# Row sums of a sliding attention by matrix products, and its outputs scaled after the product with the values

## The chip, the cores and the metric

The kernel runs on one core of a Trainium2 chip. The metric is the device time of one execution in microseconds (us), the median of several runs. A core has five engines with a queue of instructions each, which are worked off in order: PE (TensorE, matrix products into the PSUM banks, with PEld for its weight loads), DVE (VectorE), ACT (ScalarE), POOL (GpSimd) and SP, which only issues transfers. An engine waits for another through semaphores: `wait_ge(G["name"], n)` holds the queue until the counter `name` has come to n, and `.then_inc(G["name"], 1)` counts it up when an instruction is done.

## The reference, cut to what matters

The kernel computes a decoder of two layers on x of 4 batches x 256 tokens x 256 features. Only the first step of the first layer is changed, a causal attention over a sliding window, with 16 heads of width 16:

```python
qkv = x @ w_qkv.T                       # then split into q, k, v: 16 heads x 16
diff = C + qa[:, None] - ka[None, :]    # C = WINDOW = 64, keys of the chunk before and of this one
base = (diff >= 0) & (diff <= WINDOW)
scores = jnp.einsum('bhncd,bhnkd->bhnck', qc, kc) * SCALE
scores = jnp.where(mask[None, None], scores, -jnp.inf)
attn = jax.nn.softmax(scores, axis=-1)
out = jnp.einsum('bhnck,bhnkd->bhncd', attn, vc)
o = out.transpose(0, 2, 1, 3).reshape(B, S, E)
return o @ w_out.T
```

Behind it come the sum with x and a layer norm, an attention over a context of 1601 rows (below: stage B), a quantised feed-forward, and the second layer.

## The kernel before, in words

**Tiling.** The sliding attention is cut into 16 groups n = 0 to 15. Batch b has four of them, n = 4b + i, where i stands for half f of the heads (8 heads) and half t of the tokens (128 tokens). One group is a tile `sm[:, n % 4]` of 128 queries x 8 heads x 128 keys in single precision (fp32). Four such tiles are kept, and two tiles `PT` of turned weights.

**One group before the change.** PE's `a_scores(n)` writes the scores into banks 0 to 3. DVE's `a_mask(n)` adds the mask and moves them to `sm`, and `a_max(n)` takes the negated row maxima. ACT takes eight exponentials in place, one for each head, each with `accum_out` for its row sums. DVE's `a_rinv(n)` inverts the sums, and POOL multiplies the 128 x 1024 weights by them. PE's `a_transpose(n)` turns them into banks 4 and 5; DVE (i = 0 and 3) or ACT (i = 1 and 2) copies them to `PT` in `a_weightsT(n)`; PE's `a_output(n)` multiplies them with the values into bank 7.

**Once a batch.** ACT's `a_outT(b)` copies bank 7 to `oT`. PE's `a_project_out(b)` multiplies it with the output weights, again into bank 7. DVE's `a_ln(b)` adds x and takes the statistics; POOL's `rstd_of` raises the variance to the power -0.5; DVE's `ln_end` scales. PE's `a_query`, `a_key` and `a_value` project the next batch, and `to_xT` turns the normed rows.

**Order.** All engines run a loop over n written out by hand; what stands in an engine's queue has its turn in that order. DVE's loop before is

```python
a_mask(n)
if n >= 1:
    a_rinv(n - 1)
a_max(n)
if n >= 2 and not on_act(n - 2):
    a_weightsT(n - 2)
if i == 3 and b > 0:
    a_ln(b - 1)
```

so the maxima of group n stand behind the inversion for group n - 1, which waits for its eight exponentials. PE runs the scores of n, a projection, the output of n - 3 and the transposes of n - 2. Behind the loop PE projects the queries, keys and values of stage B, while ACT and DVE split the context into a high and a low part (`c_split`); then come the scores of stage B with DVE's `b_max`, ACT's `b_exp` and so on.

Of the kernel before, what the change touches and what calls it, by code (L numbers as in the profile page):

```python
# [39 lines left out]
P = 128  # L40
# [98 lines left out]
def build(nc, d, xs, ys, out):  # L139
    with ExitStack() as ctx:  # L140
# [120 lines left out]
        def w_qrT(h):  # L261
# [102 lines left out]
        rsum = sb("rsum", [P, 4, H0F])  # L364
        rinv = sb("rinv", [P, 4, H0F])
# [12 lines left out]
            a_q a_k a_v a_q_sb a_k_sb a_v_sb a_vmix a_s a_add a_max a_exp a_rinv a_norm  # L378
            a_pt a_pt_act a_pt_dve a_o a_o_sb a_y a_y_sb ld_rest
            b_q b_k b_v hi_part lo_part c_Thi c_Tlo c_Rhi c_Rlo wk_split b_s b_max b_exp b_t b_pt_hi b_pt b_o b_o_sb b_ot b_ot_sb b_y  # L380
            x_k x_neg x_exp x_kf x_kf_hi x_kf_lo x_m1 x_m1_sb x_m1T x_m1T_sb x_kv x_kvbd
# [53 lines left out]

        def on_act(n):

            return n % GROUPS in (1, 2)
# [8 lines left out]
        def _(sp):  # L447
# [31 lines left out]
            sp.wait_ge(G["const_set"], 6)  # L479
# [72 lines left out]
        def _(pool):  # L552
# [4 lines left out]
            g.memset(mhalf[:, :], -0.5).then_inc(G["const_set"], 1)  # L557

# [23 lines left out]
            def a_mixed_values(b):  # L582
# [3 lines left out]
                pool.wait_ge(G["a_norm"], GROUPS * b + 1)  # L586
                for j, (w, lo, hi) in enumerate(((1, 0, WIN), (0, WIN, P))):
                    g.tensor_copy(real(2, lo, hi), real(w, lo, hi)).then_inc(G["a_vmix"], 1)
                    pool.wait_ge(G["a_vmix"], 2 * b + j + 1)

            for n in range(NG):
# [78 lines left out]
            def r_scatter(b, parts):  # L670
                pool.wait_ge(G["r_rows"], 2 * b + 2)
                pool.wait_ge(G["ln_done"], 4 * NT + 2 * b + 2)
                if b == 0:
                    pool.wait_ge(G["const_set"], 10)
# [50 lines left out]
        def _(act):  # L725
# [47 lines left out]
            for n in range(NG):  # L773
                b, i = divmod(n, GROUPS)
                act.wait_ge(G["a_max"], n + 1)
                for h in range(H0F):
                    a.activation(sm[:, n % 4, h, :], sm[:, n % 4, h, :], ACT.Exp, bias=mx[:, n % 4, h:h + 1],  # L777
                                 accum_out=rsum[:, n % 4, h:h + 1]).then_inc(G["a_exp"], 1)
# [6 lines left out]
                if i == 1:  # L785
                    if b > 0:
                        a_outT(b - 1)
# [47 lines left out]
            def x_exp(n):  # L835
# [6 lines left out]
                a.activation(low, PS[KBANKS[c % 4]][:, 0:words], ACT.Relu, scale=-1.0).then_inc(G["x_neg"], 1)  # L842
                act.wait_ge(G["x_neg"], n + 1)
# [29 lines left out]
            for b in range(B):  # L873
                if b > 0:
                    b_oT(2 * b - 1)
                if b == 0:
                    a_outT(B - 1)
# [1728 lines left out]
```

## Time and profile before

| | |
|---|---|
| median of 3 runs | 735.99 us (735.14 to 736.39) |
| the profiled execution, its own time | 735.17 us |
| its span in the profile | 733.3 us |
| busy share of the span: PE, PEld, DVE, ACT, POOL | 89%, 73%, 66%, 59%, 27% |
| groups of the sliding attention: first scores to the first scores of stage B | 10.7 to 97.07 us |
| mean granted TensorE clock of the whole execution | 0.968 of full speed |

The span runs from the first to the last instruction that the profiler saw; the execution's own time is 1.9 us more. A row of a timeline gives the start, the duration, the engine, the line and what was written and read; in square brackets stands how long the engine had idled before it and who released it. Neighbouring instructions of an engine overlap by some tens of ns, so what one of a row of them costs is read from start to start. An fp32 matrix product is recorded as two or more instructions. All of PE's instructions have the line of a helper, so they are told apart by shapes: `32*128 32x256` are scores of an even group (t = 0), `32*64 32x256` of an odd one, `cst,arena 128*128 128x128` eight transposes, `128*32 128x128` the output of an even group, `128*32 128x64` of an odd one.

### The profile page before, as it was taken

To read this page: it belongs to the slowest core of one execution; us is meant where nothing else is said; L and a number is where in the kernel's file an instruction comes from. 1 tells how busy PE (TensorE), PEld (TensorE's weight loads), DVE (VectorE), ACT (ScalarE), POOL (GpSimd) and SP (SyncE) were. 2 spreads that over 40 slices of the span, in tenths; PEclk is the share of its full clock that TensorE was granted. 3 is DMA by queue.
4 is the path that set the end of the run, shared out by engine and by line. 5 is a ranking of instruction groups with operands and counts; after the bars stand their busy time and mean duration, and the time that the engine had idled before them with its cause. 6 is when DMAs were issued, how large, how long until landed. Compare 5 with 4: busy or idle time off the path is not lost.

```text
span 733.3 us, 13912 instructions
## 1 busy us (share of the span) xinstructions
PE 650.4 (89%) x4832; PEld 534.9 (73%) x4833; DVE 486.5 (66%) x1091; ACT 435.2 (59%) x1124; POOL 201.6 (27%) x354
## 2 busy tenths in 40 slices
PE   7798787998998999978989999999978799999950
PEld 5566677998998899864567788888865388787840
DVE  2577777469478478448877857666556577777725
ACT  4998856358357368356878747465342356566612
POOL 2455520032000000001233444344127222222315
PEclk9999899999999999998999999999999999999985
DMA  8997000220230232410020000000195201111114
GB/s 298 383 321 219 1 1 1 90 91 1 91 91 0 91 103 103 136 37 1 1 87 1 2 1 2 1 1 1 43 427 213 65 30 51 50 50 50 49 58 138
DMA packets 32226, 62.03 MB, mean 85 GB/s; under 512 B 2500, under 2 KB 26824, under 8 KB 29928
## 3 DMA queue, kind: packets, MB, share of 16 engines
q1 hardware_dynamic: 30152, 56.04, 22.6%
q0 software_dynamic: 2016, 5.22, 2.0%
q8 instruction: 36, 0.59, 0.4%
q14 instruction: 22, 0.18, 0.1%
HBM read 45.80 MB, written 15.55 MB: 84 GB/s over the span
## 4 chain that ended last, share of the span: by engine, by line
PE 68%; DVE 12%; ACT 12%; issue 3%; POOL 2%; DMA 2%; SPq 0%; POOLq 0%; ACTq 0%; DVEq 0%
PE banks L1783 45%; PE bank L1783 23%; ACT arena L777 4%; DVE U_split L1253 3%; ACT U_split L796 2%; DVE mx L1207 1%; DVE wabs L1386 1%; DMA ys<-arena 1%; POOL rstd L574 1%; ACT xT L731 1%; ACT arena L842 1%; DMA w_qkv<-in_w_qkv 1%; DVE fh L1436 1%; ACT arena L950 1%; ACT arena L997 0%
## 5 line engine op out<-in xcount | busy, mean ns | idle before, releaser
L1783 PE MATMUL banks<-U_split 128*128 128x512 f32 (+1 forms) x616 | 146.7, 350 | 5.9 <-DVE U_split L1253 3.9
L1783 PE MATMUL bank<-U_split 128*128 128x256 f32 (+1 forms) x864 | 113.1, 287 | 12.4 <-DVE U_split L1253 11.7
L1783 PEld LDWEIGHTS bank<-U_split 128*128 128x128 f32 x864 | 106.7, 191 | 15.7 <-issue 7.5
L1783 PEld LDWEIGHTS banks<-U_split 128*128 128x128 f32 x616 | 96.5, 190 | 23.6 <-issue 7.9
L796 ACT ACTIVATE U_split<-arena 128x1024 fp32r (+6 forms) x122 | 97.1, 822 | 22.0 <-DVE arena L1344 11.1
L1783 PE MATMUL banks<-cst,arena 128*128 128x128 f32 (+1 forms) x594 | 90.6, 280 | 6.1 <-DVE arena L1215 3.1
L1783 PE MATMUL banks<-arena 128*128 (+4 forms) x632 | 85.3, 386 | 4.8 <-DVE arena L1201 3.9
L571 POOL TENSOR_SCALAR rstd<-mv 128x1 f32<-128x1 f32 x38 | 10.8, 285 | 263.2 <-DVE mv L1185 239.8
L1783 PEld LDWEIGHTS banks<-cst,arena 128*128 128x128 f32 (+1 forms) x594 | 69.7, 143 | 18.5 <-POOL arena L602 3.7
L1783 PEld LDWEIGHTS banks<-arena 64*128 64x128 f32 (+3 forms) x632 | 61.5, 178 | 22.5 <-issue 7.6
L1043 ACT ACTIVATE arena<-banks,dmx 128x128 f32<-128x128 f32 (+1 forms) x128 | 52.8, 423 | 38.6 <-DVE dmx L1540 38.6
L647 POOL TENSOR_SCALAR arena<-arena,dri 128x128 f32<-128x128 f32 (+1 forms) x128 | 52.0, 425 | 75.3 <-DVE dri L1511 75.3
L1253 DVE TENSOR_TENSOR w_x_split<-arena,U_split 128x1024 fp32r<-128x1024 f32 x46 | 56.1, 1222 | 22.8 <-ACT U_split L796 22.8
L1783 PE MATMUL banks<-w_x_split,U_split 128*128 128x256 f32 (+2 forms) x196 | 66.1, 337 | 0.0
L796 ACT ACTIVATE U_split<-banks 128x512 fp32r<-128x512 f32 (+2 forms) x67 | 32.4, 505 | 54.5 <-PE banks L1783 54.5
L1253 DVE TENSOR_TENSOR U_split<-arena,U_split 128x512 fp32r<-128x512 f32 (+5 forms) x76 | 55.5, 752 | 2.3 <-ACT U_split L796 2.1
L777 ACT ACTIVATE arena<-arena,mx 128x128 f32<-128x128 f32 x128 | 49.5, 391 | 9.5 <-DVE mx L1207 9.5
L1253 DVE TENSOR_TENSOR U_split<-banks,U_split 128x512 fp32r<-128x512 f32 (+2 forms) x63 | 35.2, 571 | 27.2 <-ACT U_split L796 27.2
L713 POOL DMA_INDIRECT ys<-arena x23 | 26.2, 1140 | 95.3 <-ACT arena L1112 88.8
L1783 PE MATMUL bank<-arena 128*32 128x64 f32 (+4 forms) x672 | 46.2, 290 | 4.0 <-DVE arena L1215 1.8
L1783 PEld LDWEIGHTS bank<-arena 128*32 128x32 f32 (+2 forms) x672 | 29.3, 127 | 19.3 <-issue 5.6
L602 POOL TENSOR_TENSOR arena<-arena,rinv 128x1024 f32<-128x1024 f32 x16 | 30.4, 1899 | 43.8 <-DVE rinv L1211 43.8
(239 smaller groups left out, 1187.5 us busy)
## 6 DMA issues: line engine op xcount, KB each, us to landing
arena<-in_w_exp SPq DMA_DIRECT2D x8, 1536.0 KB, 14.1
xs<-arena SPq DMA_DIRECT2D x8, 1032.0 KB, 14.0
arena<-in_ctxT SPq DMA_DIRECT2D x4, 1601.0 KB, 6.8
arena<-in_ctx SPq DMA_DIRECT2D x4, 1536.0 KB
arena<-in_w_f SPq DMA_DIRECT2D x3, 1024.0 KB, 11.6
arena<-xs SPq DMA_DIRECT2D x23, 129.0 KB, 2.0
w_x<-in_w_x SPq DMA_DIRECT2D x9, 256.0 KB, 7.1
arena<-in_w_oh SPq DMA_DIRECT2D x1, 2048.0 KB, 8.6
```

The lines of the kernel that those rows point to most:

```text
L571: g.tensor_scalar(rstd[:, s:s + 1], mv[:, s, 1:2], LN_EPS, None, ALU.add).then_inc(G["pool_step"], 1)
L574: g.tensor_tensor(rstd[:, s:s + 1], rstd[:, s:s + 1], mhalf[:, 0:1], ALU.pow).then_inc(G["pool_step" if centre else "ln_rstd"], 1)
L602: g.tensor_tensor(sm[:, n % 4, :, :], sm[:, n % 4, :, :], rinv[:, n % 4, :].unsqueeze(2).broadcast_to([P, H0F, P]), ALU.mult).then_inc(G[" ...
L647: g.tensor_scalar(dp[:, h % 6, a:z, :], dp[:, h % 6, a:z, :], dri[:, h % 8, j:j + 1], 1.0, ALU.mult, ALU.mult).then_inc(G["d_norm"], 1)
L713: g.indirect_dma_start(ys, bass.IndirectOffsetOnAxis(ap=y_ids[:, place:place + 1], axis=0), yt[:, slot, :], None).then_inc(G[f"m_st{slot}" ...
L731: a.activation(xT[:, :, b * S:(b + 1) * S], PS_xT(stage, b)[:, :].rearrange("p (k t) -> p k t", k=KT), ACT.Copy).then_inc(G["xT_done"], 1)
L777: a.activation(sm[:, n % 4, h, :], sm[:, n % 4, h, :], ACT.Exp, bias=mx[:, n % 4, h:h + 1], accum_out=rsum[:, n % 4, h:h + 1]).then_inc(G[ ...
L796: a.activation(r32(out), src, ACT.Copy, **k).then_inc(G[s], 1)
L842: a.activation(low, PS[KBANKS[c % 4]][:, 0:words], ACT.Relu, scale=-1.0).then_inc(G["x_neg"], 1)
L1043: a.activation(dp[:, h % 6, at:z, :], score_bank(h)[:, at * P:z * P].rearrange("p (c k) -> p c k", k=P), ACT.Exp, bias=dmx[:, h % 8, j:j + ...
L1253: v.tensor_tensor(r32(out), src, r32(high).bitcast(F32), ALU.subtract).then_inc(G[s], 1)
L1783: return nc.tensor.matmul(o, w, x, start=start, stop=stop, **k)
```

## The change

The exponentials lose `accum_out`; `a_rinv` and POOL's multiplication are gone, and `a_transpose(n)` waits for the exponentials instead. The row sums come from a new function `a_sums(n)` on PE: products of the turned, unscaled weights `PT` with a constant of ones and zeros (`halves`), so that each of the 16 rows of a head in the layout of `oT` holds that head's sum for each query. They go to the upper halves of banks 0 and 1 (bank 6 for the last batch). DVE's `a_sum_copy` moves 128 x 128 of them into `oT`, POOL's `a_sum_inverse` raises them to the power -1 in place, and the copy of the outputs, which ACT made, becomes a product with them on DVE (`a_outT`). Sums and copies come at n + 4, and `a_project_out` moves behind the transposes. Counts of `const_set` that only follow from five more memsets are left out below, and so is a semaphore of stage B that was merged with another (`x_neg` into `x_exp`).

```diff
+        def sums_bank(n):
+            b, i = divmod(n, GROUPS)
+            f, t = divmod(i, TPB)
+            return PS[6][:, i * P:(i + 1) * P] if b == B - 1 else PS[f][:, 2 * P + t * P:2 * P + (t + 1) * P]
...
@@ POOL
+            def a_sum_inverse(n):
+                i = n % GROUPS
+                f, t = divmod(i, TPB)
...
+                pool.wait_ge(G["a_z_sb"], n + 1)
+                z = oT[:, f, t * P:(t + 1) * P]
+                g.tensor_tensor(z, z, mone[:, 0:1].broadcast_to([P, P]), ALU.pow).then_inc(G["a_zinv"], 1)
 
             for n in range(NG):
                 b, i = divmod(n, GROUPS)
                 if i == 1:
                     a_mixed_values(b)
+                if n >= 4:
+                    a_sum_inverse(n - 4)
                 if i == 0 and b > 1:
                     for t in range(TPB):
                         rstd_of(2 * (b - 2) + t)
...
-                pool.wait_ge(G["a_rinv"], n + 1)
-                g.tensor_tensor(sm[:, n % 4, :, :], sm[:, n % 4, :, :],
-                                rinv[:, n % 4, :].unsqueeze(2).broadcast_to([P, H0F, P]), ALU.mult).then_inc(G["a_norm"], 1)
+            for n in range(NG - GROUPS, NG):
+                a_sum_inverse(n)
@@ ACT
-            def a_outT(b):
-                act.wait_ge(G["a_o"], b + 1)
-                if b > 0:
-                    act.wait_ge(G["a_y"], b)
-                a.activation(oT, PS[7][:, :].rearrange("p (k t) -> p k t", k=KT), ACT.Copy).then_inc(G["a_o_sb"], 1)
...
                 for h in range(H0F):
-                    a.activation(sm[:, n % 4, h, :], sm[:, n % 4, h, :], ACT.Exp, bias=mx[:, n % 4, h:h + 1],
-                                 accum_out=rsum[:, n % 4, h:h + 1]).then_inc(G["a_exp"], 1)
+                    a.activation(sm[:, n % 4, h, :], sm[:, n % 4, h, :], ACT.Exp,
+                                 bias=mx[:, n % 4, h:h + 1]).then_inc(G["a_exp"], 1)
@@ DVE
-            def a_rinv(n):
-                dve.wait_ge(G["a_exp"], H0F * (n + 1))
-                v.reciprocal(rinv[:, n % 4, :], rsum[:, n % 4, :]).then_inc(G["a_rinv"], 1)
+            def a_sum_copy(n):
+                b, i = divmod(n, GROUPS)
+                f, t = divmod(i, TPB)
+                dve.wait_ge(G["a_z"], n + 1)
+                if i == 0 and b > 0:
+                    dve.wait_ge(G["a_y"], b)
+                v.tensor_copy(oT[:, f, t * P:(t + 1) * P], sums_bank(n)).then_inc(G["a_z_sb"], 1)
+
+            def a_outT(b):
+                dve.wait_ge(G["a_o"], b + 1)
+                dve.wait_ge(G["a_zinv"], GROUPS * (b + 1))
+                v.tensor_tensor(oT, PS[7][:, :].rearrange("p (k t) -> p k t", k=KT), oT, ALU.mult).then_inc(G["a_o_sb"], 1)
...
                 a_mask(n)
-                if n >= 1:
-                    a_rinv(n - 1)
+                if n >= 4:
+                    a_sum_copy(n - 4)
                 a_max(n)
+                if i == 3 and b > 0:
+                    a_outT(b - 1)
                 if n >= 2 and not on_act(n - 2):
                     a_weightsT(n - 2)
...
+            dve.wait_ge(G["a_z"], NG - 1)
+            for n in range(NG - GROUPS, NG - 1):
+                a_sum_copy(n)
             b_split_q(0)
             b_split_k(0)
             b_split_v(0)
             a_weightsT(NG - 1)
+            a_sum_copy(NG - 1)
             for b in range(B):
+                if b == 0:
+                    a_outT(B - 1)
                 b_max(2 * b, features=0 if b else 3)
@@ PE
+            def a_sums(n):
+                b, i = divmod(n, GROUPS)
...
+                pe.wait_ge(*pt_done(n))
+                if b == B - 1:
+                    pe.wait_ge(G["xT_done"], B - 2)
+                    pe.wait_ge(G["a_z_sb"], NG - GROUPS if n < NG - 1 else n)
+                o = sums_bank(n)
+                for j in range(2):
+                    for r in range(QUADS):
+                        ins = mm(o[r * D0P:(r + 1) * D0P, :], halves[:, j, :], PT[:, n % 2, 2 * r + j, :], start=j == 0, stop=j == 1,
+                                 tile_position=(0, r * D0P))
+                ins.then_inc(G["a_z"], 1)
...
                 if n > 0:
                     pe.wait_ge(G["a_add"], n)
+                if n >= 5:
+                    pe.wait_ge(G["a_z_sb"], n - 4)
+                if n >= 4:
+                    a_sums(n - 4)
...
             def a_transpose(n):
-                pe.wait_ge(G["a_norm"], n + 1)
+                pe.wait_ge(G["a_exp"], H0F * (n + 1))
...
-                if i == 3 and b > 0:
-                    a_project_out(b - 1)
...
+                if n == NG:
+                    a_sums(n - 4)
                 if i == 0 and n > 0:
                     a_output(n - 4)
+                if n >= NG:
+                    a_sums(n - 3)
                 if n >= 3 and (n - 3) % GROUPS > 0:
                     a_output(n - 3)
                 if n >= 2:
                     a_transpose(n - 2)
+                if i == 3 and b > 0:
+                    a_project_out(b - 1)
...
                     if (b, c) == (0, 2):
+                        a_sums(NG - 1)
                         a_output(NG - 1)
```

Where the change moves instructions is shown at three places. The first is PE from the scores of group 7 on. Before:

```order
L1783 MATMUL banks<-arena 64x256 x8
L1783 MATMUL bank<-arena 128x256 x4
L1783 MATMUL banks<-cst,arena 128x128 x8
L1783 MATMUL banks<-arena 128x256 x4
L1783 MATMUL bank<-w_qkv,xT 128x256 x4
L1783 MATMUL bank<-arena 32x128 x8
L1783 MATMUL bank<-arena 32x64 x16
```

PE from the scores of group 7 on, of the changed kernel:

```order
L1811 MATMUL banks<-arena 64x256 x8
L1811 MATMUL banks<-cst,arena 128x128 x8
L1811 MATMUL bank<-arena 128x256 x4
L1811 MATMUL banks<-arena,halves 32x128 x8
L1811 MATMUL banks<-arena 128x256 x4
L1811 MATMUL bank<-w_qkv,xT 128x256 x4
L1811 MATMUL bank<-arena 32x128 x8
L1811 MATMUL bank<-arena 32x64 x16
```

The project-out (`bank<-arena 128x256`) has moved behind the eight transposes of group 5, and the sums of group 4 (`halves`) stand ahead of the scores of group 8. The second place is DVE from the mask of group 7 on. Before:

```order
L1201 TENSOR_TENSOR arena<-banks,cst 128x1024
L1211 RECIPROCAL rinv<-rsum 128x8
L1207 TENSOR_REDUCE mx<-arena 128x8
L1224 TENSOR_TENSOR res<-bank,x_ids 128x256 x2
L1227 BN_STATS stats<-res 128x6 x2
L1230 BN_AGGR mv<-stats 128x2 x2
L1201 TENSOR_TENSOR arena<-banks,cst 128x1024
```

DVE from the mask of group 7 on, of the changed kernel:

```order
L1213 TENSOR_TENSOR arena<-banks,cst 128x1024
L1227 COPY arena<-banks 128x128
L1219 TENSOR_REDUCE mx<-arena 128x8
L1232 TENSOR_TENSOR arena<-bank,arena 128x512
L1245 TENSOR_TENSOR res<-bank,x_ids 128x256 x2
L1248 BN_STATS stats<-res 128x6 x2
L1251 BN_AGGR mv<-stats 128x2 x2
L1213 TENSOR_TENSOR arena<-banks,cst 128x1024
```

The inversion has gone, the copy of group 3's sums stands in its place, and the product for the outputs (L1232) stands ahead of the layer norm's rows. The third place is POOL from the first group's weights on. Before:

```order
L602 TENSOR_TENSOR arena<-arena,rinv 128x1024
L588 COPY arena<-arena 64x8x2x16 x2
L602 TENSOR_TENSOR arena<-arena,rinv 128x1024 x4
L588 COPY arena<-arena 64x8x2x16 x2
L602 TENSOR_TENSOR arena<-arena,rinv 128x1024 x3
```

POOL behind its first transfer, of the changed kernel:

```order
L598 COPY arena<-arena 64x8x2x16 x2
L608 TENSOR_TENSOR arena<-arena,mone 128x128
L598 COPY arena<-arena 64x8x2x16 x2
L608 TENSOR_TENSOR arena<-arena,mone 128x128 x4
L582 TENSOR_SCALAR rstd<-mv 128x1
```

Sixteen multiplications of 128 x 1024 have become sixteen powers of 128 x 128, four groups later.

## Rows read from the trace of the kernel before

**Rows 1.** Chain that ended last, 0 to 140 us: shares by line

```profile
by line: ACT arena L777 22.2%; PE bank L1783 16.2%; PE banks L1783 15.8%; DVE mx L1207 5.7%; DVE U_split L1253 5.5%; issue 4.1%; ACT U_split L796 3.4%; DMA w_qkv<-in_w_qkv 2.6%; ACT arena L767 2.1%; DVE arena L1201 1.8%; POOL rstd L574 1.7%
```

**Rows 2.** Waits, 0 to 130 us: total us, times, longest us

```profile
DVE rinv L1211 <- ACT arena L777: 20.5, 14, 3.0
```

**Rows 3.** DVE's timeline: start, us, what, idle before

```profile
21.83 0.20 DVE L1211 RECIPROCAL rinv<-rsum 128x8 f32<-128x8 f32 x1 [2.12 <-ACT arena L777]
...
46.71 0.74 DVE L1224 TENSOR_TENSOR res<-bank,x_ids 128x256 f32<-128x256 f32 x2
...
60.16 0.20 DVE L1211 RECIPROCAL rinv<-rsum 128x8 f32<-128x8 f32 x1 [0.99 <-ACT arena L777]
60.28 1.17 DVE L1207 TENSOR_REDUCE mx<-arena 128x8 f32<-128x1024 f32 x1
61.36 1.21 DVE L1215 COPY arena<-banks 128x1024 f32<-128x1024 f32 x1
62.49 1.21 DVE L1201 TENSOR_TENSOR arena<-banks,cst 128x1024 f32<-128x1024 f32 x1
```

**Rows 4.** Windows from scores to scores of groups 0, 4, 8, 12, stage B

```profile
10.70:26.27 15.57, 9.33 (x82) 6.43 (x81) 9.54 (x10) 11.72 (x52) 4.57 (x4) 0.94 1.07 374
26.27:44.50 18.23, 17.18 (x210) 12.44 (x209) 12.04 (x14) 16.26 (x67) 8.37 (x6) 0.96 1.06 372
44.50:63.89 19.39, 17.06 (x212) 12.60 (x213) 14.26 (x22) 17.04 (x73) 9.96 (x10) 1.00 1.10 314
63.89:88.08 24.19, 17.46 (x254) 13.11 (x253) 17.11 (x30) 19.78 (x85) 12.88 (x15) 0.86 0.19 52
```

In Rows 4 the columns are: window, its length, busy us (and instructions) of PE, PEld, DVE, ACT, POOL, granted TensorE clock, DMA share, GB/s.

**Rows 5.** ACT's timeline, two of the eight exponentials of group 9

```profile
56.93 0.40 ACT L777 ACTIVATE arena<-arena,mx 128x128 f32<-128x128 f32 x1 [1.90 <-DVE mx L1207]
57.24 0.19 ACT L777 ACTIVATION_READ_ACCUMULATOR arena<-arena,mx 128x1 f32 x1
57.33 0.39 ACT L777 ACTIVATE arena<-arena,mx 128x128 f32<-128x128 f32 x1
```

**Rows 6.** PE's timeline: scores, outputs, transposes, stage B

```profile
24.39 1.94 PE L1783 MATMUL banks<-cst,arena 128*128 128x128 f32 x8 [3.12 <-DVE arena L1215]
26.27 1.24 PE L1783 MATMUL banks<-arena 32*128 32x256 f32 x8
...
35.14 0.65 PE L1783 MATMUL bank<-arena 128*32 128x128 f32 x16
35.71 1.09 PE L1783 MATMUL banks<-cst,arena 128*128 128x128 f32 x8
...
44.50 0.71 PE L1783 MATMUL banks<-arena 32*128 32x256 f32 x8
...
63.89 0.71 PE L1783 MATMUL banks<-arena 32*128 32x256 f32 x8
...
93.13 1.89 PE L1783 MATMUL banks<-w_x,xT 128*128 128x256 f32 x8
97.07 3.08 PE L1783 MATMUL banks<-U_split 128*128 128x512 f32 x12 [2.05 <-DVE U_split L1328]
```

**Rows 7.** DVE's groups of like shapes: busy us, mean ns

```profile
L1401 DVE COPY arena<-bank 128x257 f32<-128x257 f32 x8 | 3.0, 415 | 0.0
L1562 DVE TENSOR_TENSOR arena<-arena,cst 128x128 f32<-128x128 f32 x4 | 1.2, 292 | 0.1
```

**Rows 8.** POOL's lines: ns min/median/max; the last row: busy us, mean ns

```profile
L571 POOL TENSOR_SCALAR rstd<-mv x38: 202/216/1235, 52.3 to 728.5; 128x1 f32<-128x1 f32 x38
L661 POOL TENSOR_SCALAR rstd<-mv x5: 227/231/365, 529.6 to 559.6; 128x2 f32<-128x2 f32 x5
L574 POOL TENSOR_TENSOR rstd<-rstd,mhalf x38: 547/567/1531, 52.6 to 728.8; 128x1 f32<-128x1 f32 x38
L664 POOL TENSOR_TENSOR rstd<-rstd,mhalf x5: 706/717/734, 529.9 to 560.0; 128x2 f32<-128x2 f32 x5
...
L602 POOL TENSOR_TENSOR arena<-arena,rinv 128x1024 f32<-128x1024 f32 x16 | 30.4, 1899 | 43.8 <-DVE rinv L1211 43.8
```

More of the change, by code:

```diff
@@ L363, in build @@
         mx = sb("mx", [P, 4, H0F])
-        rsum = sb("rsum", [P, 4, H0F])
-        rinv = sb("rinv", [P, 4, H0F])
+        halves = sb("halves", [P, 2, D0P])
+        mone = sb("mone", [P, 1])
         bmx = sb("bmx", [P, 8])
@@ L477, in _ @@
                 load(w_f32[:, n, :], d[f"w_f{n}"], "ld_ffn_lat")
-            sp.wait_ge(G["const_set"], 6)
+            sp.wait_ge(G["const_set"], 11)
             xs_tiles = xs.rearrange("(t p) e -> p t e", p=P)
@@ L557, in _ @@
             g.memset(mhalf[:, :], -0.5).then_inc(G["const_set"], 1)
+            g.memset(halves[:, 0, 0:D0], 1.0).then_inc(G["const_set"], 1)
+            g.memset(halves[:, 0, D0:D0P], 0.0).then_inc(G["const_set"], 1)
+            g.memset(halves[:, 1, 0:D0], 0.0).then_inc(G["const_set"], 1)
+            g.memset(halves[:, 1, D0:D0P], 1.0).then_inc(G["const_set"], 1)
+            g.memset(mone[:, :], -1.0).then_inc(G["const_set"], 1)
             pool.wait_ge(G["const_set"], 2)
@@ L673, in r_scatter @@
                 if b == 0:
-                    pool.wait_ge(G["const_set"], 10)
+                    pool.wait_ge(G["const_set"], 15)
                 for n in parts:
@@ L785, in _ @@
                 if i == 1:
-                    if b > 0:
-                        a_outT(b - 1)
                     if b + 1 < B:
@@ L841, in x_exp @@
                 low = kf_lo[:, n % 3, 0:words]
-                a.activation(low, PS[KBANKS[c % 4]][:, 0:words], ACT.Relu, scale=-1.0).then_inc(G["x_neg"], 1)
-                act.wait_ge(G["x_neg"], n + 1)
+                a.activation(low, PS[KBANKS[c % 4]][:, 0:words], ACT.Relu, scale=-1.0).then_inc(G["x_exp"], 1)
+                act.wait_ge(G["x_exp"], 2 * n + 1)
                 a.activation(low, low, ACT.Exp, scale=-1.0).then_inc(G["x_exp"], 1)
@@ L876, in _ @@
                 if b == 0:
-                    a_outT(B - 1)
+                    act.wait_ge(G["a_o"], B)
                 x_exp(CP * b)
@@ L1016, in e_gate @@
                 if b == 0:
-                    act.wait_ge(G["const_set"], 11)
+                    act.wait_ge(G["const_set"], 16)
                 for k in range(KT):
@@ L1025, in e_exp @@
                     act.wait_ge(G["e_qf"], b - 1)
-                a.activation(eq[:, b % 2, :], PS[QUERY_BANKS[b]][:, :], ACT.Relu, scale=-1.0).then_inc(G["x_neg"], 1)
-                act.wait_ge(G["x_neg"], CP * B + b + 1)
+                a.activation(eq[:, b % 2, :], PS[QUERY_BANKS[b]][:, :], ACT.Relu, scale=-1.0).then_inc(G["x_exp"], 1)
+                act.wait_ge(G["x_exp"], 2 * CP * B + b + 1)
                 a.activation(eq[:, b % 2, :], eq[:, b % 2, :], ACT.Exp, scale=-1.0).then_inc(G["e_exp"], 1)
@@ L1245, in _ @@
                         ln_end(2 * (b - 2) + t)
-            a_rinv(NG - 1)
             for t in range(TPB):
@@ L1340, in x_features @@
                 words = 2 * E if n % CP < CP - 1 else E
-                dve.wait_ge(G["x_exp"], n + 1)
+                dve.wait_ge(G["x_exp"], 2 * n + 2)
                 k1 = kf_lo[:, n % 3, 0:words]
@@ L1832, in a_value @@
                 ins.then_inc(G["a_v"], 1)
+            def a_sums(n):
+                b, i = divmod(n, GROUPS)
+                if n == 0:
+                    pe.wait_ge(G["const_set"], 8)
+                pe.wait_ge(*pt_done(n))
[8 more added lines that the diff above has]
+                ins.then_inc(G["a_z"], 1)
             def a_scores(n):
@@ L2022, in x_keys @@
                     pe.wait_ge(G["xT_done"], B)
-                    pe.wait_ge(G["const_set"], 8)
+                    pe.wait_ge(G["const_set"], 13)
                 else:
@@ L2134, in _ @@
                     pe.wait_ge(G["xT_done"], B - 2)
+                    pe.wait_ge(G["a_z_sb"], NG)
                     to_xT(0, B - 2)
```

7 lines of the change are left out of this document (4 added, 3 removed).

## The prediction, on record before the changed kernel ran

> **What bounds the kernel now.** I read the chain that ended last first, then the waits, then DVE's and PE's timelines, then the windows by batch. Up to 140 us the exponentials hold the largest share of the chain, 22.2%, with PE's rows behind them [rows 1]. The reason is a ring through DVE's order: the inversion for group n-1 waits for its eight exponentials, the maxima of group n stand behind it, and ACT needs these for its next eight. The wait is there 14 times, 20.5 us in all [rows 2]. Around 60 us one turn reads: inversion at 60.16 after 0.99 us idle, maxima at 60.28, weights copy at 61.36, next mask at 62.49 [rows 3]. The change cuts this ring.
>
> But the windows say that a second engine stands right behind. In batch 1 PE is busy 17.18 of 18.23 us, in batch 2 17.06 of 19.39; only in batch 0 (9.33 of 15.57) and batch 3 (17.46 of 24.19, at a clock of 0.86) is there room [rows 4]. So the question is what the change puts on PE.
>
> **ACT: removed.** The accumulator read starts 0.31 us after its exponential and the next exponential 0.09 us later, 0.40 from start to start for the pair shown, about 0.385 over the eight [rows 5]. Without the read I take 0.30 each, so a group falls by 8 x 0.09 = 0.7 us, 2.9 us a batch. The outputs' copy, once a batch, goes too. ACT was busy 16.3 of 18.23 us in batch 1 [rows 4]; at some 13 us it bounds nothing. Bounds of this term: no saving (the read is hidden) to 0.2 us a head (the read's whole 0.19); by neither does ACT come to hold the ring, so the sum does not hang on it.
>
> **PE: added.** `a_sums` is eight products of 128 columns with 32 output rows, the form of an even group's output: from that output's start at 35.14 to the transposes at 35.71 it is 0.57 us [rows 6]. I take 0.58; 16 times makes 9.3 us, 2.3 in a full batch. Nothing is taken off PE.
>
> **DVE.** Each group loses the inversion (0.12 from start to start) with its wait, and gains a copy of 128 x 128. Nearest rows: 0.415 us for 257 columns out of PSUM, 0.292 for 128 columns in SBUF [rows 7]; from start to start I take 0.2 (bounds 0.12 and 0.42). The product `a_outT` is of 512 columns: half of a 1024-column pass, 1.13 from start to start, so 0.6. A group is then mask 1.2, copy 0.2, maxima 1.1 and in every second group the weights copy 1.13 [rows 3].
>
> **POOL: the dear unknown.** Sixteen multiplications of 1.9 us go, sixteen powers of 128 x 128 come. The trace has powers of one and two columns only: 567 and 717 ns, 150 ns for the second column [rows 8]. A simple operation shows that such a second column says little of a long row: one column takes 216 ns, two 231, that is 15 ns more, whereas 1024 columns take 1899 ns, under 1.9 a column [rows 8]. The lower end is a power whose columns cost no more than the multiplication's: 0.57 + 127 x 0.00186 = 0.8 us. The upper is 150 ns a column: 0.57 + 127 x 0.15 = 19.6 us. Between them I scale by the same ratio as the simple operation, 1.9/15, or an eighth: 150 falls to 19 ns and the power to 3.0 us; with the whole two-input pass as the measure (1.9 us for eight times the columns) it is 0.8. I take 1.6 us, P below, about the geometric middle of these two, and keep 0.8 and 19.6 for the rivals and the range.
>
> The GPSIMD Engine Reference of the Trainium skill (Elementwise, side-by-side cycle accounting) counts about 2.6 cycles a column for a two-input operation, which agrees with the 1.9 ns row. By that rule, as an estimate, a power of 128 columns would be about 0.57 + 0.28 = 0.85 us, and the sum below would come to about 1 us instead of 2; the page states no price for a power itself, so it may be far off.
>
> **PE's new wait.** Ahead of `a_project_out` in groups 7, 11 and 15 stands a chain that was not there: scores end, mask 1.2, copy 0.2, power P beside the maxima (1.1), product 0.6 and some 0.2 of hops: 2.2 + P, if P is over 1.1. PE covers 1.0 of it with eight transposes (35.71: 1.09 us) and 0.4 more with the four of `to_xT` from batch 2 on [rows 6]. With P = 1.6 PE idles 2.8, 2.4 and 2.4 us. Behind PE's waiting project-out stand the next sums and scores, behind DVE's product its weights copy, the layer norm and the next mask.
>
> **The sum, by batch**, against the windows [rows 4]:
> - Batch 0: no sums yet, and the ring is open. Before, DVE idled 2.12 us before 21.83, turned to the first weights copy only after the maxima, and PE sat 3.12 us until 24.39 and then ran at the low clock level (eight transposes 1.94 us) [rows 3, 6]. Now the copy starts when the first transposes end at about 20.1, so ends at 21.3; transposes 21.4 to 22.5, sums 0.6, scores of group 4 at 23.1 instead of 26.27: -3.2.
> - Batch 1: 17.2 + 2.3 + 2.8 = 22.3 instead of 18.23: +4.1.
> - Batch 2: 17.1 + 2.3 + 2.4 and 0.2 of small waits = 22.0 instead of 19.39: +2.6.
> - Batch 3 has only the value projection, so DVE leads: scores of group 12 to mask 13 6.1 (0.7 scores, 1.9 values, 1.2 outputs, 1.0 transposes, 0.6 sums, 0.7 scores), two steps of 3.75 (1.2 + 0.2 + 1.1 + 1.13 and hops), then 1.2 + 0.2 + 1.6 + 0.65 to the end of the product, 1.85 project-out, 0.7 for DVE's two adds (46.71 [rows 3]) and 2.8 for two outputs, one more sum and eight transposes on PE. That is 22.6 instead of 24.19: -1.6.
> - Into stage B: PE is 1.9 late and has 0.6 more for the sums of group 14, so its value projection ends at 95.0 + 2.5 = 97.5. Before it ended at 93.13 + 1.89 and PE then waited 2.05 for DVE until 97.07 [rows 6]; that wait now hides all but 0.4. DVE's three copies (0.6) and the shorter exponentials cancel. The sums of group 15 add 0.6 between the scores of stage B: +1.0 in all.
> - One of the three new PE waits, 2.4 to 2.8 us long, I expect to cost clock, as the wait of 3.12 us did: 0.9 us, what those transposes took over 1.04 [rows 6]. +0.9.
>
> Total +1.9 us. The profiled execution takes 735.17 (span 733.3 and 1.9 around it), 0.8 under the median; 735.17 + 1.9 = 737.1 there, and 737.9 against the median of 735.99. I forecast **737.9 us**.
>
> **The rivals.** I call it no change within 0.2%, 1.5 us, about what a measurement of this kernel can tell.
> - *The forecast's case*: PE full, P near 1 to 2.5, from 734.5 to 742. Chance 0.48, of which 0.19 within 1.5 us of before.
> - *Faster*: PE's wait is hidden. If copy, power and product end within the transposes, the three waits (7.6 us) shrink; for it speaks that P may be 0.8 and that batches 1 and 2 had 1.0 and 2.3 us of idle PE in which sums fit [rows 4]; and no low clock at all would save 0.9. It decides when the wait falls under 1.6 us a batch: 1.2 off each makes -3.6, without clock cost -0.9, and 1.9 - 4.5 = -2.6; with fuller overlap of products -5. About 732. Against it: mask, copy and product alone are 2.0. Chance 0.24.
> - *The power is a good deal slower*, P from 2.5 to 8 us, so POOL sets the end. At P = 3 the three waits grow by 1.4 each, and the last product waits for four powers in a row from about 99.5 us: ends 112 and DVE's maxima of stage B 9 us late: 745. At P = 6 POOL needs 24 us a batch and pauses 5 us in each between product and next copy: about +40, 776. Chance 0.13.
> - *150 ns for every column*, P = 19.6: sixteen in a row are 314 us from 25 us on, with pauses some 360 before stage B goes on instead of 100: +260, 996 us. Nothing in the rows excludes it but the simple operation's example. Chance 0.11.
> - *The exponentials don't get shorter*: 0.385 stays. ACT has 16 us of work in a batch of 22, so the sum moves by under 1 us: 738.5. Chance 0.04.
>
> **The numbers.** Faster 0.24. Same 0.19, and 0.01 from the last rival: 0.20. Slower 0.29 + 0.13 + 0.11 + 0.03 = 0.56. The range leaves out the 19.6 us power (0.11), half of the middle one (P over about 3.7) and 0.03 below: 730 to 752. The likeliest case's own range is 734.5 to 742.
>
> The skill's page TensorE: Matmul & The Clock Gate (The HAM clock gate) says that an idle array falls to 1.2 GHz; the row at 24.39 agrees (1.94 us against 1.09 for the same eight transposes) [rows 6]. [...]
>
> **What the profile of the changed kernel would show.** Right: no DVE wait for L777's successor ahead of the maxima, exponentials 0.30 apart, eight sum products in 0.58 us, PE idle 2 to 3 us ahead of each project-out with DVE as releaser, scores of group 4 near 23, of 8 near 45.5, of 12 near 67, stage B's first near 97.5. Wrong: a power over 2.5 us, or POOL busy through the stage; a PE wait under 1.6 us, which turns the sign; PE windows of batches 1 and 2 under 20 us, which would mean that the sums don't add their 2.3. The likeliest error is P; the next is the clock, which in batch 3 stood at 0.86 and could come back to full or fall elsewhere.

## The result

The changed kernel takes 1028.38 us (median of 4 runs, 1027.73 to 1029.36) against 735.9 us, a ratio of 1.398 (95% interval 1.396 to 1.401). The forecast was 737.9 us with a range of 730 to 752: wrong by 290 us, though the direction was the likelier one. The fourth case, 150 ns for every column and 996 us, had been given a chance of 0.11.

The page of the changed kernel: share of the chain by line, the costliest group, and who waited for it (section 4, then section 5: busy us, mean ns, idle us before and its releaser).

```profile
POOL arena L608 32%; PE banks L1811 31%; PE bank L1811 17%; DVE U_split L1275 2%; ACT U_split L808 2%; POOL rstd L585 1%; DVE wabs L1414 1%; DMA w_qkv<-in_w_qkv 1%; DMA ys<-arena 1%; DVE arena L1213 0%; POOL rstd L582 0%; ACT arena L854 0%; ACT arena L962 0%; DVE fh L1464 0%; ACT arena L1009 0%
...
L608 POOL TENSOR_TENSOR arena<-arena,mone 128x128 f32<-128x128 f32 x16 | 331.3, 20726 | 38.3 <-DVE arena L1227 38.2
...
L1232 DVE TENSOR_TENSOR arena<-bank,arena 128x512 f32<-128x512 f32 x4 | 2.8, 692 | 251.0 <-POOL arena L608 251.0
```

L608 is the power. One takes 20.7 us, sixteen 331.3 us, and DVE's four products of the outputs (L1232) wait 251 us for them. POOL's timeline shows that the powers run one behind the other until DVE can hand out the next sums:

```profile
26.47 20.77 POOL L608 TENSOR_TENSOR arena<-arena,mone 128x128 f32<-128x128 f32 x1 [13.16 <-DVE arena L1227]
...
48.14 62.10 POOL L608 TENSOR_TENSOR arena<-arena,mone 128x128 f32<-128x128 f32 x3
118.04 20.71 POOL L608 TENSOR_TENSOR arena<-arena,mone 128x128 f32<-128x128 f32 x1 [7.80 <-DVE arena L1227]
...
142.61 62.12 POOL L608 TENSOR_TENSOR arena<-arena,mone 128x128 f32<-128x128 f32 x3 [1.17 <-DVE arena L1227]
...
313.88 82.80 POOL L608 TENSOR_TENSOR arena<-arena,mone 128x128 f32<-128x128 f32 x4 [6.64 <-DVE arena L1227]
```

And DVE's timeline shows the last product and the first maxima of stage B behind it:

```profile
396.79 0.69 DVE L1232 TENSOR_TENSOR arena<-bank,arena 128x512 f32<-128x512 f32 x1 [77.92 <-POOL arena L608]
397.39 1.68 DVE L1296 TENSOR_REDUCE bmx<-banks 128x1 f32<-128x512 f32 x3
```

In the kernel before it stood here:

```profile
99.27 0.67 DVE L1274 TENSOR_REDUCE bmx<-banks 128x1 f32<-128x512 f32 x1
```

The first maximum of stage B has moved from 99.27 to 397.39 us, 298.1 us later. The spans differ by 293.2, so behind that point the changed kernel is 4.9 us shorter. PE is busy there for 566.30 us instead of 571.21, so that much of its work had been done while it waited. So the whole loss lies ahead of that point. What PE did meanwhile is read from a window between the transposes ahead of the first project-out and DVE's first product: busy for 0.19 of 69.34 us (the columns are those of [rows 4]).

```profile
41.00:110.34 69.34, 0.19 (x2) 0.00 (x0) 1.56 (x3) 3.47 (x9) 69.10 (x6) 0.52 0.43 123
```

The part before the first product waits went as the hand-made schedule said. PE's timeline shows the sums of group 0 in 0.57 us from start to start, and the scores of group 4 behind them at 24.08. This execution's scores of group 0 started 1.0 us later than before's, so that is 23.1, as forecast, against 26.27 before [rows 6]. The project-out then comes after a wait of 69.90 us:

```profile
23.51 0.64 PE L1811 MATMUL banks<-arena,halves 128*32 128x128 f32 x16
24.08 0.71 PE L1811 MATMUL banks<-arena 32*128 32x256 f32 x8
...
40.12 1.06 PE L1811 MATMUL banks<-cst,arena 128*128 128x128 f32 x8 [0.22 <-DVE arena L1236]
111.09 3.78 PE L1811 MATMUL bank<-arena 128*128 128x256 f32 x8 [69.90 <-DVE arena L1232]
```

### The profile page after: what moved, and what is told of

Read it like the earlier page. It is cut to its first block, busy times and chain, and to the rows that moved or that the text cites. A ratio compares the mean times of both kernels' runs of the same rounds, so it can differ in the third digit from the quotient of the medians.

```text
span 1026.5 us, 14318 instructions
## 1 busy us (share of the span) xinstructions
PE 667.9 (65%) x5088; PEld 545.6 (53%) x5089; DVE 490.4 (48%) x1095; ACT 421.4 (41%) x992; POOL 500.5 (49%) x359
## 4 chain that ended last, share of the span: by engine, by line
PE 48%; POOL 34%; DVE 8%; ACT 5%; issue 2%; DMA 2%; SPq 0%; POOLq 0%; ACTq 0%; DVEq 0%
POOL arena L608 32%; PE banks L1811 31%; PE bank L1811 17%; DVE U_split L1275 2%; ACT U_split L808 2%; POOL rstd L585 1%; DVE wabs L1414 1%; DMA w_qkv<-in_w_qkv 1%; DMA ys<-arena 1%; DVE arena L1213 0%; POOL rstd L582 0%; ACT arena L854 0%; ACT arena L962 0%; DVE fh L1464 0%; ACT arena L1009 0%
## 5 line engine op out<-in xcount | busy, mean ns | idle before, releaser
L608 POOL TENSOR_TENSOR arena<-arena,mone 128x128 f32<-128x128 f32 x16 | 331.3, 20726 | 38.3 <-DVE arena L1227 38.2
L1811 PE MATMUL bank<-arena 128*32 128x64 f32 (+4 forms) x672 | 52.8, 301 | 253.9 <-DVE arena L1232 253.3
L1811 PEld LDWEIGHTS bank<-arena 128*32 128x32 f32 (+2 forms) x672 | 33.4, 133 | 269.5 <-DVE arena L1232 254.3
L1232 DVE TENSOR_TENSOR arena<-bank,arena 128x512 f32<-128x512 f32 x4 | 2.8, 692 | 251.0 <-POOL arena L608 251.0
L781 ACT ACTIVATE arena<-banks 128x1024 f32<-128x1024 f32 x8 | 8.2, 1022 | 196.9 <-PE banks L1811 196.9
L1811 PEld LDWEIGHTS banks<-arena 64*128 64x128 f32 (+3 forms) x632 | 61.7, 180 | 20.5 <-issue 8.7
L1275 DVE TENSOR_TENSOR w_x_split<-arena,U_split 128x1024 fp32r<-128x1024 f32 x46 | 56.1, 1222 | 23.1 <-ACT U_split L808 23.1
L791 ACT ACTIVATE arena<-arena,mx 128x128 f32<-128x128 f32 x128 | 39.1, 393 | 42.4 <-DVE mx L1219 42.4
```

The lines of the kernel that those rows point to most:

```text
L608: g.tensor_tensor(z, z, mone[:, 0:1].broadcast_to([P, P]), ALU.pow).then_inc(G["a_zinv"], 1)
L781: a.activation(PT[:, n % 2, :, :], PS_T[:, :, :].rearrange("p w (h q) -> p (w h) q", q=P), ACT.Copy).then_inc(G["a_pt_act"], 1)
L1275: v.tensor_tensor(r32(out), src, r32(high).bitcast(F32), ALU.subtract).then_inc(G[s], 1)
L1811: return nc.tensor.matmul(o, w, x, start=start, stop=stop, **k)
```

## The experiments

Times are medians; ratios are to the kernel before on the same chip, with 95% intervals. Where two runs on different chips are compared, the difference of their ratios is given beside that of the medians.

**The price of a power, by itself.** The kernel before, with this behind POOL's last work:

```diff
+            for w in (1, 2, 4, 8, 16, 32, 64, 128):
+                for op, c in ((ALU.pow, scx), (ALU.mult, ones)):
+                    scratch(g.tensor_tensor(scr[:, 0:w], scr[:, 0:w], c[:, 0:1].broadcast_to([P, w]), op))
```

> The kernel before, with powers to -1 and multiplications by 1 of 1, 2, 4, 8, 16, 32, 64 and 128 columns on a scratch tile put behind POOL's last work, each waiting for the one ahead, to measure them by themselves (some 45 us are added to the end). A cost for every column: 0.41 + 0.16 us a column, so 0.57, 0.73, 1.05, 1.7, 3.0, 5.5, 10.6, 20.9 us. What the prediction leaned on, that the second column is dearer than the later ones: a bend in the list. For the multiplication, the kernel with it in the power's place has 0.40 us at 128 columns, so hardly any step from width to width.

POOL's timeline of this kernel (`scr<-scr,scx` is the power, `scr<-scr,ones` the multiplication):

```profile
730.74 0.56 POOL L733 TENSOR_TENSOR scr<-scr,scx 128x1 f32<-128x1 f32 x1
...
731.64 0.70 POOL L733 TENSOR_TENSOR scr<-scr,scx 128x2 f32<-128x2 f32 x1
732.42 0.20 POOL L733 TENSOR_TENSOR scr<-scr,ones 128x2 f32<-128x2 f32 x1
732.69 1.02 POOL L733 TENSOR_TENSOR scr<-scr,scx 128x4 f32<-128x4 f32 x1
...
734.07 1.64 POOL L733 TENSOR_TENSOR scr<-scr,scx 128x8 f32<-128x8 f32 x1
...
739.33 5.42 POOL L733 TENSOR_TENSOR scr<-scr,scx 128x32 f32<-128x32 f32 x1
...
745.14 10.52 POOL L733 TENSOR_TENSOR scr<-scr,scx 128x64 f32<-128x64 f32 x1
...
756.12 20.73 POOL L733 TENSOR_TENSOR scr<-scr,scx 128x128 f32<-128x128 f32 x1
776.92 0.40 POOL L733 TENSOR_TENSOR scr<-scr,ones 128x128 f32<-128x128 f32 x1
```

This is one execution. There is no bend: 0.40 us and 0.159 us for every column describe all eight widths. The multiplication goes from 0.19 to 0.40 us. The second column added 0.14 us, and each of the last 64 added 0.16 (10.52 to 20.73 us).

**Half the columns.** The power over the first 64 of the 128 columns; the other half stays uninverted.

```diff
-                g.tensor_tensor(z, z, mone[:, 0:1].broadcast_to([P, P]), ALU.pow).then_inc(G["a_zinv"], 1)
+                g.tensor_tensor(z[:, 0:P // 2], z[:, 0:P // 2], mone[:, 0:1].broadcast_to([P, P // 2]), ALU.pow).then_inc(G["a_zinv"], 1)
```

> The changed kernel with the power over the first 64 of the 128 columns only, the other half left uninverted. If POOL's power costs the same for every column (160 ns), one takes 0.4 + 64 x 0.16 = 10.6 us and POOL's sixteen still set the end of the stage: the time falls by 16 x 10.2 = 163 us to about 865 us. If a large fixed part hides in the 20.7 us, one takes clearly more than 11 us and the time falls by less.

Measured: 865.9 us, ratio 1.175 (1.171 to 1.179), one power 10.53 us (ns min/median/max):

```profile
L608 POOL TENSOR_TENSOR arena<-arena,mone x16: 10515/10526/10576, 25.9 to 223.3; 128x64 f32<-128x64 f32 x16
```

Against 1028.38 that is 162.5 us less, and 16 x (20.72 - 10.53) is 163.0. At these widths every microsecond of power is a microsecond of the kernel.

**A multiplication in the power's place**, all waits kept; the outputs aren't normalised.

```diff
-                g.tensor_tensor(z, z, mone[:, 0:1].broadcast_to([P, P]), ALU.pow).then_inc(G["a_zinv"], 1)
+                g.tensor_tensor(z, z, mone[:, 0:1].broadcast_to([P, P]), ALU.mult).then_inc(G["a_zinv"], 1)
```

> The changed kernel with POOL's power turned into a multiplication by the same constant, all waits and places kept; the sums aren't inverted, so the outputs aren't normalised. Theory A (the 16 powers of 20.7 us in a row are the whole loss, everything else of the change costs the +1 to +2 us of the prediction's sum): 736 to 738 us, PE idle 2 to 2.5 us ahead of each project-out, project-outs 22 to 23 us apart. Rival B (the new order itself, sums on PE and the waits through DVE and POOL, costs much more than thought): over 745 us. Rival C (with a cheap inverse the open ring wins, as the change means it): under 733 us.

Measured: 735.48 us, ratio 1.000 (0.997 to 1.003). The median falls just under theory A's 736 to 738 and by its interval agrees with it; B and C fall. So without the power the rest of the change, its gains and its costs together, comes to nothing within 0.3%. The median hides a spread: of twelve executions, the six with a mean clock of 0.977 to 0.981 take 732.7 to 734.9 us, the five with 0.968 to 0.970 take 738.3 to 742.0. The profiled one (740.0 us) belongs to these, and its PE timeline shows where: each project-out comes after some 2 us of waiting for DVE's product and takes 3.4 instead of 1.99 us.

```profile
42.67 3.48 PE L1811 MATMUL bank<-arena 128*128 128x256 f32 x8 [2.03 <-DVE arena L1232]
...
65.78 3.42 PE L1811 MATMUL bank<-arena 128*128 128x256 f32 x8 [1.85 <-DVE arena L1232]
...
86.27 3.42 PE L1811 MATMUL bank<-arena 128*128 128x256 f32 x8 [1.90 <-DVE arena L1232]
```

The granted clock over the first of them, from 42.67 to 46.10 us, is 0.56 of full speed, so nine tenths of it at 1.2 GHz:

```profile
42.67:46.10 3.43, 3.42 (x11) 2.54 (x11) 0.00 (x0) 1.83 (x7) 0.00 (x0) 0.56 1.09 299
```

**The power over 8 columns**, one 1.64 us: the value with which the forecast's sum was made. The other 120 columns stay uninverted. The edit is that of the half, with 8 for `P // 2`.

> The changed kernel with the power over 8 of the 128 columns, the rest left uninverted: P = 1.65 us by the widths measured alone, the value that the prediction's sum was made with (1.6). Theory A (only the price of the power was wrong, the sum around it holds): 737.9 us within 2, and 1 to 6 us over the kernel with the multiplication (P = 0.40), since the wait ahead of each of three project-outs grows by at most 0.6 us (P is 1.1 us beside the maxima) and they may run at the lower clock. Rival B (the sum around it is wrong too): under 734 or over 742.

Measured: 741.63 us, ratio 1.007 (1.006 to 1.009): 3.7 over the forecast, outside A's 2 and just short of B. The three project-outs stand here, with their waits:

```profile
43.35 3.78 PE L1811 MATMUL bank<-arena 128*128 128x256 f32 x8 [2.81 <-DVE arena L1232]
...
68.57 2.54 PE L1811 MATMUL bank<-arena 128*128 128x256 f32 x8 [2.63 <-DVE arena L1232]
...
89.74 3.22 PE L1811 MATMUL bank<-arena 128*128 128x256 f32 x8 [2.68 <-DVE arena L1232]
```

The first wait is as forecast (2.8 us), the other two are 0.2 and 0.3 us over the forecast's 2.4. The low clock is not as forecast: 3.78 + 2.54 + 3.22 against three times 1.99 is 3.6 us on the project-outs alone, where the sum had 0.9 in all. And it goes on behind them, in the sums and the scores:

```profile
48.08 1.24 PE L1811 MATMUL banks<-arena 32*128 32x256 f32 x8
...
51.23 1.09 PE L1811 MATMUL bank<-arena 128*32 128x128 f32 x48
```

From the first project-out to these outputs it is 7.88 us; the same row of instructions at full clock takes 5.07 (42.76 to 47.83 in the kernel with the product ahead of the maxima, below). The second stretch takes 6.59 us instead of 5.06 (64.13 to 69.19), and the third, up to the transposes, 5.62 instead of 4.39 (83.95 to 88.34). That is 5.6 us of low clock, 4.7 more than the sum's 0.9. The profiled execution, 741.61 us, lies 4.5 over the 737.1 that the prediction gave for it.

Against the kernel with the multiplication it is 6.1 us more by the medians and 5.5 by the ratios, at the upper end of the 1 to 6 expected.

**The reciprocal on DVE.** All is computed. The copy of the sums becomes the reciprocal, and POOL's part goes.

```diff
-                v.tensor_copy(oT[:, f, t * P:(t + 1) * P], sums_bank(n)).then_inc(G["a_z_sb"], 1)
+                v.reciprocal(oT[:, f, t * P:(t + 1) * P], sums_bank(n)).then_inc(G["a_z_sb"], 1)
...
-                dve.wait_ge(G["a_zinv"], GROUPS * (b + 1))
+                dve.wait_ge(G["a_z_sb"], GROUPS * (b + 1))
```

> The changed kernel with the inverse taken by DVE: the copy of 128 x 128 sums becomes a reciprocal into the same place, POOL has none of it; all is computed. Nearest rows: reciprocals of 8 and 32 columns take 202 and 353 ns, 6.3 ns a column, so 0.96 us for 128 instead of the copy's 0.28, 0.7 us more on DVE for each group, but no hop over POOL ahead of the project-out. Theory A: about the time of the run with the multiplication, within 1.5 us: 736 to 739 us. Rival B: over 745. Rival D (DVE becomes the bound by 16 x 0.7 us): 11 us over the run with the multiplication, 748.

Measured: 745.15 us, ratio 1.010 (1.008 to 1.013); one reciprocal 0.948 us, as worked out. That is more than theory A gave and just over B's bound, but under D's 748. Two places that differ are seen in the profiled execution (740.89 us, the fastest of six). The wait ahead of the project-outs is 2.46 to 2.64 us; one of the three runs at the low clock, in 3.68 us, the other two in 1.99. Four of the six have a mean clock of 0.972 or less and take 745.0 to 745.5; that their project-outs ran at the low clock more often is likely, but they have no trace. And three reciprocals stand ahead of the split queries of stage B, for which PE then waits 2.13 us instead of 0.29. DVE's timeline, then PE's:

```profile
96.11 3.70 DVE L1271 TENSOR_TENSOR U_split<-arena,U_split 128x1024 fp32r<-128x1024 f32 x4 [0.16 <-ACT U_split L804]
99.73 2.57 DVE L1223 RECIPROCAL arena<-bank 128x128 f32<-128x128 f32 x3
102.22 0.63 DVE L1346 SCALAR_TENSOR_TENSOR U_split<-banks,U_split 128x512 fp32r<-128x512 f32 x1
...
102.91 3.43 PE L1807 MATMUL banks<-U_split 128*128 128x512 f32 x8 [2.13 <-DVE U_split L1346]
```

**The product ahead of the maxima.** The same kernel, all computed, with the order in DVE's loop changed:

```diff
-                a_max(n)
                 if i == 3 and b > 0:
                     a_outT(b - 1)
+                a_max(n)
```

> The kernel with the reciprocal on DVE, and with DVE's product of the outputs ahead of the maxima of groups 7, 11 and 15 instead of behind them; all is computed. PE's idle time ahead of each project-out was 2.46 to 2.64 us there. Theory A (copy, inverse and product stand in the way of the project-out through DVE's order): the wait falls by the 1.1 us of the maxima to about 1.4 us, three times, and if the project-outs stay at full clock (1.99 us instead of 3.68 in one of them) by up to 1.7 us more: 3 to 5 us under the kernel with the reciprocal, about 741. Rival B (PE's own 9 us of added sums are the cost, the waits are not): within 1.5 us of it, 744 to 746.

Measured: 737.22 us, ratio 1.003 (1.000 to 1.005). Under the kernel with the reciprocal that is 7.9 us by the medians, but 5.4 by the ratios and 2.2 between the two profiled executions, so about the 3 to 5 expected. The waits fell from 2.46 to 2.64 us to 1.6 to 1.8. In the profiled execution (738.71 us) all three project-outs stayed at full clock, but the first scores of stage B, behind the wait of 2.13 us that is still there, took 4.61 us, where they took 3.08 before [rows 6]:

```profile
42.76 1.99 PE L1807 MATMUL bank<-arena 128*128 128x256 f32 x8 [1.76 <-DVE arena L1228]
...
47.83 1.09 PE L1807 MATMUL bank<-arena 128*32 128x128 f32 x48
...
98.78 4.61 PE L1807 MATMUL banks<-U_split 128*128 128x512 f32 x12 [2.13 <-DVE U_split L1346]
```

Rival B falls: the waits do cost time. What PE's added sums cost isn't priced by this pair, since both kernels have all of them.

**Half of the sum products.** On the kernel with the multiplication: `for j in range(1)` for `range(2)` in `a_sums`, with start and stop both set, so half of the heads are left out of the sums.

> The kernel with POOL's multiplication in the power's place, and with four of the eight sum products for each group (the second heads of each pair are left out of the sums; the outputs aren't normalised). It prices the change's addition on PE: 16 x 0.29 = 4.6 us less. Theory A (PE holds the pace in batches 1 and 2): some 2.3 to 4 us less than with all eight, 731.5 to 733.5 us. Rival B (PE's sums fit into idle time): within 1 us of it.

Measured: 734.25 us, ratio 0.997 (0.996 to 0.998). The kernel with all eight has a median of 735.48, a gap of 1.2 us, near B; by the ratios it is 2.1, between B and A. The clock blurs it: that kernel's executions fall into two groups and this one's don't (732.45 to 735.15, mean clock 0.972 to 0.975). The profiled one runs two of three project-outs in 1.99 us and one in 2.60. Also, half of the sum products still take 0.35 us a group from start to start instead of 0.57, so 3.5 us of work went and not the 4.6 expected. Batch 1 alone can be compared in the traces: 21.06 us here, at full clock, against 23.11 with all eight, of which 1.5 are the low clock (6.56 instead of 5.07 us from the first project-out to the outputs behind it). So there four groups' 0.9 us less of products is worth about 0.6. What it is worth over the whole stage stays open.

**The maxima ahead of the inversion.** The kernel before, all computed, with one order changed and no part of the change:

```diff
                 a_mask(n)
+                a_max(n)
                 if n >= 1:
                     a_rinv(n - 1)
-                a_max(n)
```

> The kernel before, with DVE's inversion for group n - 1 moved behind the maxima of group n, and nothing else: accumulators, inversion and POOL's multiplication stay. It opens the ring through the exponentials without the sums on PE; all is computed. Theory A (the ring was worth what DVE waited in it, and PE is the next bound): ACT then has 17.2 us of work in a batch and PE 17.1, so batches take about 17.5 instead of 18.2 and 19.4 us, and batch 0 gains 2 to 3 us: 728 to 732 us. Rival B (PE and the turned weights hold the pace anyway, opening the ring gives nothing): 734.5 to 737.5.

Measured: 732.07 us, ratio 0.994 (0.992 to 0.996), at the upper end of theory A. In the traces stage B's first scores come 83.41 us after those of group 0, before 86.37 [rows 6], so the gain lies in this stage. DVE waits for exponentials 9 times for 10.3 us instead of 14 times for 20.5 [rows 2]:

```profile
DVE rinv L1211 <- ACT arena L777: 10.3, 9, 3.7
```

Part of the gain may be clock: six of these ten executions have a mean clock of 0.978 to 0.981, and only three of 21 of the kernel before on the same chip, which take 732.0 to 732.4 us. How much of the 3.7 us comes by it isn't separated.

**No accumulators.** The kernel before without `accum_out`; the inversion reads a constant, so row sums are left out.

```diff
-                    a.activation(sm[:, n % 4, h, :], sm[:, n % 4, h, :], ACT.Exp, bias=mx[:, n % 4, h:h + 1],
-                                 accum_out=rsum[:, n % 4, h:h + 1]).then_inc(G["a_exp"], 1)
+                    a.activation(sm[:, n % 4, h, :], sm[:, n % 4, h, :], ACT.Exp, bias=mx[:, n % 4, h:h + 1]).then_inc(G["a_exp"], 1)
...
+            link(v.memset(rsum[:, :, :], 33.0))
```

> The kernel before with the exponentials' accumulators taken away and nothing put in their place: the inversion reads a constant, so the row sums are left out. It measures the one saving of the change on ACT by itself, inside the ring. Theory A (0.09 us a head): each turn of the ring shortens by 0.7 us, 16 x 0.7 = 11 us at most, less where PE bounds: 727 to 731 us. Rival B (the read is hidden, or PE takes it all): 734.5 to 737.5.

Measured: 727.7 us, ratio 0.990 (0.988 to 0.993). Theory A holds, and so does its price: eight exponentials take 2.45 us, the last one's 0.39 included, so 0.295 from start to start instead of about 0.385 (0.40 for the pair in [rows 5]).

```profile
42.56 2.45 ACT L777 ACTIVATE arena<-arena,mx 128x128 f32<-128x128 f32 x8
```

**Both parts together**, the row sums left out as there.

> The kernel before with both single parts: no accumulators (the inversion reads a constant, row sums left out), and the inversion behind the maxima. It asks how far ACT and the ring can be eased before PE stops it. The parts alone gave -8 and -4 us. Theory A (PE, 17.1 us of work a batch, is right behind): clearly less than the sum of both, 724 to 728 us. Rival B (they add up): 722 to 724 or under.

Measured: 726.91 us, ratio 0.988 (0.985 to 0.990). Against the kernel before on their chips the parts gave 8.0 and 3.7 us, together 9.4, so the order adds 1.4 to what the accumulators give. By the ratios it is 7.1 and 4.4, together 9.2. The time lies in theory A's range, and outside B's; but the gap between the sum of the parts and both, 2.3 us, is within what the three intervals leave open. For A speaks the trace of the fastest execution (723.41 us; the others take 726.76 to 727.96): scores of groups 4 and 8 stand at 23.03 and 40.43, a batch of 17.4 us, and PE was busy for 17.18 us in that batch before [rows 4]:

```profile
23.03 0.71 PE L1783 MATMUL banks<-arena 32*128 32x256 f32 x8
...
40.43 0.71 PE L1783 MATMUL banks<-arena 32*128 32x256 f32 x8
```

## Why the prediction was wrong, by its own steps

- **The step that failed is the price of the power.** The prediction wrote that "a simple operation shows that such a second column says little of a long row": it took 216, 231 and 1899 ns of POOL's simple operations [rows 8], found a second column of 15 ns beside 1.9 ns a column in a long row, carried that ratio over to the power, and came to 3.0, then 1.6 us. Measured alone, a power has no such bend: 0.40 us and 0.159 us a column. The plain line through the two rows it had, 567 and 717 ns, gave 19.6 us for 128 columns, 5% under the 20.7 measured, and stood in the text as the upper end. A chance of 0.11 for a plain reading of the only two rows of the very operation was far too small. Also, the simple operations compared were two kinds (a scalar operation of one and two columns, a product of 1024); for a product the list shows 0.19 us at one column and 0.20 at two, four and eight. The estimate of 0.85 us beside it was 24 times too low; and by the prediction's own formula, in which P counts only over 1.1 us, the sum would then have been +0.4 us, not about +1.
- **What that price does to the kernel** was right in kind. The rival's 996 us were 32 too low. It had expected the powers to start at 25 us and stage B to go on at some 360; they start at 26.47, and the first maximum stands at 397.39. Of these 37 us, 18 are 16 x 1.1 us of power, about as many are pauses (38.9 us between the powers, where some 21 had been assumed), and 1.5 the later start; 4.9 came back behind that point. The pauses are longer because each batch restarts almost from empty (7.80, 1.17 and then 6.64 us of idle before a power, and the layer norm's POOL work between).
- **ACT's term** was right: 0.30 us a head forecast, 0.295 measured. That it moves nothing in the changed kernel isn't shown, since no run has the accumulators back there; in the kernel before it is worth 7 to 8 us.
- **PE's added term** was right as a duration, 0.57 us a group. What it costs is the less certain: the half gave 1.2 to 2.1 us with the clock uncontrolled. The kernel with both single parts has the ring open and no accumulators, as the changed kernel has with the multiplication, but no sums on PE and no new wait: 726.91 against 735.48 us, 8.6 us by the medians and 9.1 by the ratios. So much do the sums, the waits and the clock behind them cost together; their shares aren't separated.
- **The new wait ahead of the project-out** was right in place and releaser, and nearly in size: 2.8, 2.6, 2.7 us with a power of 1.64 us, where 2.8, 2.4, 2.4 had been worked out.
- **The clock term** was too small. One of three waits was to be paid for with 0.9 us; at the assumed price all three were, with 5.6 us in the profiled execution, which is about the whole of its miss of 4.5. So the rest of the sum held there. The kernel before had the sign of it in batch 3, where waits of 1.81 us, shorter than the three forecast, were followed by transposes in 1.97 instead of 1.09 us:

```profile
77.42 1.08 PE L1783 MATMUL bank<-arena 128*32 128x64 f32 x32 [1.81 <-DVE arena L1215]
78.43 1.97 PE L1783 MATMUL banks<-cst,arena 128*128 128x128 f32 x8
```

- **The ring** of exponentials was real: opening it gives about 4 us by moving one line, some of it perhaps clock. With the accumulators gone it gives 1.4 us by the medians and 2.1 by the ratios. That agrees with the windows' warning that PE stands right behind, though the runs don't tell this apart from noise.

A complete kernel that is faster than both is the one with the maxima ahead of the inversion, 732.07 us. With the best of the tried placements, the change's own idea comes to 737.22 us, no faster than before. Not tried: the reciprocals of the last batch elsewhere than ahead of stage B's split, and sums on PE in a bank that DVE isn't reading, so that they could follow the outputs directly.

## What to carry to other kernels

Price an operation from its own rows, and if it is there at two sizes, take the line through them as the forecast and a bend as the rival, not the other way round; with an unknown that can be 1 or 20 us, a look at it alone is worth more than any schedule around it. A small wait of PE in a dense stage costs its own length and can then cost the clock of what follows. In the traces of four of these kernels, eight of twelve project-outs behind waits of 1.85 to 2.81 us took 2.5 to 3.8 us instead of 1.99; in a fifth, none of three behind 1.6 to 1.8 us did. Where a step that waits stands in a queue ahead of one that could run, swap them before restructuring: one line gave here what a new dataflow didn't.

## What the runs showed of the hardware that was not expected

- POOL's power costs 0.159 us for each column of 128 partitions, 0.40 us fixed, the same rate from 1 to 128 columns; a product of 128 columns takes 0.40 us in all, a fiftieth of the power's 20.73. The Trainium skill's GPSIMD Engine Reference (Elementwise, side-by-side cycle accounting) gives about 2.6 cycles an element for two-input operations. The product of 1024 columns is somewhat under that, 1.9 ns a column [rows 8], which is 2.2 cycles at the 1.2 GHz of that page; the power is at about 190, though both are the same instruction, TENSOR_TENSOR.
- DVE's reciprocal of 128 x 128 takes 0.948 us, 22 times less than POOL's power to -1.
- The mean clock of otherwise equal executions of one kernel, the one with the multiplication, fell into two groups, 0.977 to 0.981 and 0.968 to 0.970, some 7 us apart; in the traced one PE waited about 1.9 us ahead of three project-outs. The kernel before spreads too: on one chip, twelve of its executions at 0.966 to 0.968 took 735.4 to 738.6 us and eight at 0.970 to 0.979 took 732.0 to 735.7. So differences of 2 or 3 us between medians can be clock alone.
